# Decoder output product in two column pairs: one between the fourth and fifth projection of a turn, one behind the sixth

## The reference, cut to what matters

```python
x = x + _L0_xattn_ref(_layernorm(x, axis=-1), ctx_4096)          # x: (8, 64, 2048)
x = x + _L0_attn_ref(_layernorm(x, axis=-1), w_q, w_k, w_v, w_o)
x = x + _L0_ffn_ref(_layernorm(x, axis=-1), A_w, B_w, Wq_w, keys)

def _L0_attn_ref(hidden_states, w_q, w_k, w_v, w_o):              # 32 heads, 8 key groups of 4, 128 wide
    q = (hidden_states @ w_q).reshape(B, S, Hkv, g, D)
    k = (hidden_states @ w_k).reshape(B, S, Hkv, D)
    v = (hidden_states @ w_v).reshape(B, S, Hkv, D)
    scores = jnp.einsum('bqhgd,bkhd->bhgqk', q, k) * scale        # causal mask, softmax
    attn = jnp.einsum('bhgqk,bkhd->bqhgd', probs, v)
    return attn.reshape(B, S, Hq * D) @ w_o                       # (512, 4096) @ (4096, 2048)
```

## Time and profile before

| | us |
|---|---|
| median of 3 runs | 1690.09 |
| lowest, highest | 1689.28, 1690.12 |
| profiled execution, its own time | 1688.0 |
| its span, first to last instruction | 1686.1 |

### The profile page before, as it was taken

The page is one execution under the profiler, slowest core; times in us unless marked ns, Lnnn a source line. Parts: engine busy times, 40 slices in busy tenths (PEclk is TensorE's granted clock), DMA queues, the critical chain, the costliest instruction groups (busy, mean ns, idle before and its releaser), DMA issues.

```text
span 1686.1 us, 22552 instructions
## 1 busy us (share of the span) xinstructions
PE 1629.8 (97%) x8893; PEld 1196.6 (71%) x8893; DVE 765.7 (45%) x1331; ACT 554.5 (33%) x784; POOL 490.6 (29%) x155
## 2 busy tenths in 40 slices
PE   6999999999999979999999999999999999999999
PEld 5565565655556558887887878878878878887877
DVE  3464645556464360137156256263371561248433
ACT  2433433443444332233233233332332332322221
POOL 0000000000011004348458366474484583350010
PEclk9999999999999989999999999999999999999999
DMA  9556576675776514322314323224223143220023
GB/s 329 156 202 216 189 240 191 212 227 179 244 232 203 182 53 158 92 76 92 107 51 127 87 85 100 75 75 124 75 91 107 51 148 118 84 100 26 26 75 125
DMA packets 178888, 224.58 MB, mean 133 GB/s; under 512 B 4240, under 2 KB 102544, under 8 KB 176048
## 3 DMA queue, kind: packets, MB, share of 16 engines
q1 hardware_dynamic: 178816, 223.56, 41.4%
HBM read 212.54 MB, written 11.01 MB: 133 GB/s over the span
## 4 chain that ended last, share of the span: by engine, by line
PE 54%; issue 23%; POOL 18%; DVE 2%; ACT 1%; DMA 1%; POOLq 0%; SPq 0%; DVEq 0%
PE ps L623 12%; PE ps L690 11%; POOL w_lo L1149 10%; PE ps L664 10%; POOL w_lo L1156 8%; PE ps L742 5%; PE ps L744 5%; PE ps L743 5%; PE ps L1812 1%; PE ps L635 1%; DMA xa_raw_a<-in_ctx 0%; PE ps L1633 0%; PE ps L1667 0%; PE ps L668 0%; DMA raw<-in_L_attn_w_o 0%
## 5 line engine op out<-in xcount | busy, mean ns | idle before, releaser
L1149 POOL TENSOR_TENSOR w_lo<-raw,w_hi 128x2048 fp32r<-128x2048 f32 x46 | 212.2, 4612 | 421.0 <-ACT w_hi L1203 399.1
L742 PE MATMUL ps<-h_hi,w_hi 128*128 128x512 f32 x800 | 316.5, 396 | 0.0
L744 PE MATMUL ps<-h_hi,w_lo 128*128 128x512 f32 x800 | 311.8, 390 | 0.0
L743 PE MATMUL ps<-h_lo,w_hi 128*128 128x512 f32 x800 | 311.5, 389 | 0.0
L442 ACT ACTIVATE xa_ct<-ps 128x512 f32<-128x512 f32 x256 | 152.8, 598 | 186.6 <-PE ps L623 115.6
L577 DVE COPY xa_ct<-ps 128x321 f32<-128x321 f32 (+1 forms) x256 | 117.5, 459 | 210.8 <-PE ps L623 136.0
L664 PE MATMUL ps<-xa_ct,xa_q_t 128*64 128x384 f32 x1024 | 184.5, 490 | 0.0
L742 PEld LDWEIGHTS ps<-h_hi,w_hi 128*128 128x128 f32 x800 | 150.3, 188 | 35.2 <-ACT sa_q_t L1268 2.0
L744 PEld LDWEIGHTS ps<-h_hi,w_lo 128*128 128x128 f32 x800 | 150.1, 188 | 32.1
L743 PEld LDWEIGHTS ps<-h_lo,w_hi 128*128 128x128 f32 x800 | 150.4, 188 | 29.6
L1143 POOL TENSOR_TENSOR w_lo<-raw,w_hi 128x2048 fp32r<-128x2048 f32 x2 | 9.1, 4542 | 506.9 <-ACT w_hi L1043 506.9
(11 more groups left out here) (236 smaller groups left out, 2312.6 us busy)
## 6 DMA issues: line engine op xcount, KB each, us to landing
xa_raw_a<-in_ctx SPq DMA_DIRECT2D x32, 1536.0 KB
xa_raw_b<-in_ctx SPq DMA_DIRECT2D x32, 1536.0 KB, 6.7
raw<-in_L_attn_w_q SPq DMA_DIRECT2D x32, 1024.0 KB, 5.9
raw<-in_L_attn_w_o SPq DMA_DIRECT2D x30, 1024.0 KB, 5.1
raw<-in_L_attn_w_k SPq DMA_DIRECT2D x8, 1024.0 KB, 5.8
raw<-in_L_attn_w_v SPq DMA_DIRECT2D x8, 1024.0 KB, 5.8
xa_xq<-in_x SPq DMA_DIRECT2D x8, 512.0 KB, 5.1
xa_raw_a<-in_ctx SPq DMA_DIRECT2D x32, 128.0 KB
```

The costliest lines, as they stand in the source:

```text
L742: pe.matmul(out, hi, mov_hi, start=first, stop=False)
L743: pe.matmul(out, hi, mov_lo, start=False, stop=False)
L744: return pe.matmul(out, lo, mov_hi, start=False, stop=last)
L1149: pool.tensor_tensor(w_lo[:, n % 2, :], raw[:, n % 2, :], w_hi[:, n % 2, :].bitcast(F32), ALU.subtract).then_inc(w_lo_done, 1)
```

## The change

The first column pair (j = 0) is multiplied between the fourth projection (q1) and the fifth (q2), the second behind the sixth as before. Everything that feeds it is renumbered for that:

- PE: `output_parts(g, 0)` stands behind `values_transpose(g)`. The fifth and sixth projection now wait also until part 6's results are out of banks 0 and 1.
- SP: the loads come in the order k, q0, v, q1, two chunks of `w_o`, q2, q3, two chunks of `w_o`. q2's load waits for the first pair's four weight sums, q3's for part 6's low copy, and the second pair's chunks for the low copies of q2 and q3.
- ACT: parts 0 and 1 of the first pair are split behind the third projection's result, the other five behind the fourth's, then q2 in two halves and q3 (`split_between`). Parts 0, 1, 2, 6 of the second pair are split behind the fifth's and sixth's result.
- POOL: the low copies follow that order; q2's comes in two halves.
- DVE: all four weight sums of a pair stand ahead of all its additions. The fourth (p = 5) waits for part 1's low copy in place of part 6's.

`heads_high` and `head_lows` stay where they were in their engines' orders.

The diff, without the parts that only renumber:

```diff
...
@@ -981,7 +982,21 @@
-        return done0(g) + NP + PARTS * j + SPLIT_ORDER.index(p) + 1
+        return done0(g) + EARLY_P + (PARTS + 3) * j + SPLIT_ORDER.index(p) + 1
+    def item_no(g, n):
+        if isinstance(g, int) or n < EARLY_P:
+            return done0(g) + n + 1
+        return done0(g) + PARTS + n + 2
+    def load_no(g, n):
+        return n if isinstance(g, int) or n < EARLY_P else n + 2
+    def wo_load(j):
+        return EARLY_P + 4 * j
@@ -1058,9 +1073,10 @@
                     srcs.append(w_q_v[:, :, bass.ds((g * HG + int(what[1])) * HD, HD)])
-            last = isinstance(g, int) and g == LAST
-            for c in (range(n_wo) if last else (0, 2, 1, 3)[:n_wo]):
-                srcs.append(w_o_v[g - 1, :, :, c * 512:(c + 1) * 512])
+            by_parts = not isinstance(g, int)
+            last = n_wo and not by_parts
+            wo = [w_o_v[g - 1, :, :, c * 512:(c + 1) * 512] for c in ((0, 2, 1, 3) if by_parts else range(n_wo))]
+            srcs = srcs[:EARLY_P] + wo[0:2] + srcs[EARLY_P:] + wo[2:4] if by_parts else srcs + wo
             for n, src in enumerate(srcs):
@@ -1068,9 +1084,13 @@
                     sp.wait_ge(w_lo_done, done0(g))
-                elif n == NP + 2 and not last:
+                elif by_parts and n == load_no(g, EARLY_P):
                     sp.wait_ge(t_sums, 1 + TURN_SUMS * (g - 1) + 4)
-                elif n < NP + 2 or last:
+                elif by_parts and n == load_no(g, EARLY_P + 1):
+                    sp.wait_ge(w_lo_done, split_no(g, 0, PARTS - 1))
+                elif by_parts and n >= wo_load(1):
+                    sp.wait_ge(w_lo_done, item_no(g, n - wo_load(1) + EARLY_P))
+                else:
                     sp.wait_ge(w_lo_done, done0(g) + n - 1)
@@ -1144,17 +1164,28 @@
         def turn(g):
-            for n in range(2 if isinstance(g, int) and g == 0 else 0, NP):
-                pool.wait_ge(w_hi_done, done0(g) + n + 1)
-                pool.tensor_tensor(w_lo[:, n % 2, :], raw[:, n % 2, :], w_hi[:, n % 2, :].bitcast(F32),
+            def item(n, part=slice(0, D), more=0):
+                pool.wait_ge(w_hi_done, item_no(g, n) - more)
+                pool.tensor_tensor(w_lo[:, n % 2, part], raw[:, n % 2, part], w_hi[:, n % 2, part].bitcast(F32),
                                    ALU.subtract).then_inc(w_lo_done, 1)
-            if isinstance(g, int):
-                return
-            for j in range(2):
+            def blocks(j):
                 for p in SPLIT_ORDER:
...
                                        ALU.subtract).then_inc(w_lo_done, 1)
+            if isinstance(g, int):
+                for n in range(0 if g else 2, NP):
+                    item(n)
+                return
+            for n in range(EARLY_P):
+                item(n)
+            blocks(0)
+            item(EARLY_P, slice(0, HALF_D), 1)
+            item(EARLY_P, slice(HALF_D, D))
+            item(EARLY_P + 1)
+            blocks(1)
@@ -1208,16 +1239,27 @@
+        def split_between(g):
+            act.wait_ge(w_in[0], 8 * (item0(g) + load_no(g, EARLY_P)) + 16)
+            for k, p in enumerate((3, 4)):
+                act.wait_ge(wo_bank, banks0(g) + 2 * p + 2)
+                part = slice(k * HALF_D, (k + 1) * HALF_D)
+                act.activation(w_hi[:, 0, part], raw[:, 0, part], ACT.Copy).then_inc(w_hi_done, 1)
+            act.wait_ge(w_in[1], 8 * (item0(g) + load_no(g, EARLY_P)) + 16)
+            act.wait_ge(wo_bank, banks0(g) + 2 * PARTS)
+            act.activation(w_hi[:, 1, :], raw[:, 1, :], ACT.Copy).then_inc(w_hi_done, 1)
         def split_half(g, j, p):
             if p in FROM_RAW:
-                act.wait_ge(w_in[FROM_RAW[p][0]], 8 * (item0(g) + NP + 2 * j) + 16)
+                act.wait_ge(w_in[FROM_RAW[p][0]], 8 * (item0(g) + wo_load(j)) + 16)
             else:
...
             same, q = HELD_BY[p]
-            if same or j:
-                act.wait_ge(wo_bank, banks0(g) + 2 * (PARTS * (j - 1 + same) + q) + 2)
+            if same:
+                act.wait_ge(wo_bank, banks0(g) + 2 * (PARTS * j + q) + 2)
             else:
-                act.wait_ge(proj_done, NP * g + NP - 1 + PLACE_OF[p] // 2)
+                act.wait_ge(proj_done, NP * g + EARLY_P - 1 + 2 * j + PLACE_OF[p] // 2)
             act.activation(half_slot(w_hi, p), half_source(p), ACT.Copy).then_inc(w_hi_done, 1)
@@ -1283,9 +1325,13 @@
                     act.activation(keys_t[:], ps_wq[0:RD, DC * RD:DC * RD + EXPERTS], ACT.Copy).then_inc(wq_hi, 1)
-                if by_parts and n + 2 >= NP:
-                    for p in SPLIT_ORDER[2 * (n + 2 - NP):][:2]:
-                        split_half(g, 0, p)
+                if by_parts and n + 2 >= EARLY_P:
+                    for p in SPLIT_ORDER[n % 2 * 2:][:2]:
+                        split_half(g, (n + 2 - EARLY_P) // 2, p)
+                    if n == EARLY_P - 1:
+                        for p in SPLIT_ORDER[4:]:
+                            split_half(g, 0, p)
+                        split_between(g)
                 else:
@@ -1293,8 +1339,6 @@
                 for p in SPLIT_ORDER[4:]:
-                    split_half(g, 0, p)
-                for p in SPLIT_ORDER:
                     split_half(g, 1, p)
@@ -1451,7 +1495,7 @@
                 for n in range(2):
-                    dve.wait_ge(w_in[n], 8 * (item0(g) + NP + 2 * j) + 16)
+                    dve.wait_ge(w_in[n], 8 * (item0(g) + wo_load(j)) + 16)
             dve.wait_ge(w_lo_done, split_no(g, 0, p) if j else done0(g))
@@ -1463,7 +1507,7 @@
-                dve.wait_ge(w_lo_done, split_no(g, j, PARTS - 1))
+                dve.wait_ge(w_lo_done, split_no(g, j, 1))
                 dve.tensor_tensor(t1, b12, b11, ALU.subtract).then_inc(t_sums, 1)
@@ -1492,15 +1536,12 @@
             head_lows(g)
-            for p in (2, 3, 4):
-                weight_sum(g, 0, p)
-            for i in range(WO_HALVES):
-                for r2 in range(2):
-                    add_part(g, i, r2)
-                if i == 1:
-                    weight_sum(g, 0, 5)
-                if PARTS - 3 <= i <= PARTS:
-                    weight_sum(g, 1, i - PARTS + 5)
+            for j in range(2):
+                for p in (2, 3, 4, 5):
+                    weight_sum(g, j, p)
+                for i in range(PARTS * j, PARTS * (j + 1)):
+                    for r2 in range(2):
+                        add_part(g, i, r2)
@@ -1637,9 +1678,10 @@
         def project(g, n):
-            n0 = done0(g)
             slot = n % 2
-            pe.wait_ge(w_lo_done, n0 + n + 1)
+            pe.wait_ge(w_lo_done, item_no(g, n))
+            if not isinstance(g, int) and n >= EARLY_P:
+                pe.wait_ge(wo_added, evac_no(g, PARTS - 1, n - EARLY_P))
@@ -1709,9 +1751,11 @@
             if i == 0:
-                pe.wait_ge(proj_out, NP * (g + 1) - 1 + r2)
+                pe.wait_ge(proj_out, NP * g + EARLY_P - 1 + r2)
                 if r2 == 0:
                     pe.wait_ge(a_lo_done, 3 * g)
+            if i == PARTS + 1:
+                pe.wait_ge(proj_out, NP * (g + 1) - 1 + r2)
             if r2 == 0:
@@ -1745,6 +1789,11 @@
             i.then_inc(wo_bank, 1)
+        def output_parts(g, j):
+            for i in range(PARTS * j, PARTS * (j + 1)):
+                for r2 in range(2):
+                    times_w_o_part(g, i, r2)
@@ -1767,6 +1816,8 @@
             values_transpose(g)
+            if not isinstance(g, int):
+                output_parts(g, 0)
             project(g, 4)
@@ -1775,9 +1826,7 @@
             if kind(g)[1]:
-                for i in range(WO_HALVES):
-                    for r2 in range(2):
-                        times_w_o_part(g, i, r2)
+                output_parts(g, 1)
```

More of the change, by code:

```diff
@@ L758 @@
 WO_HALVES = 2 * PARTS
-TURN_W = NP + WO_HALVES
+EARLY_P = 4
+TURN_W = NP + 1 + WO_HALVES
 TURN_BANKS = 2 * WO_HALVES
```

## The result

| | before | after |
|---|---|---|
| median of 4 runs, us | 1690.11 | 1722.88 |
| lowest, highest | 1689.28, 1690.37 | 1721.76, 1724.65 |
| span of the profiled execution | 1686.1 | 1720.4 |
| mean granted clock of PE | 0.996 | 0.984 |

The changed kernel takes 1.0196 times as long (95% interval 1.0178 to 1.0213): 32.8 us slower. The forecast was 1725, with 1712 to 1739 as the range.

A forecast was written before the change was run, and what follows sets the result against it. TensorE, busy 97%, was taken as the bound, with 4.95 us a turn to win. A 6.35 + B 3.3 + C 0.9 + restarts = 10.85, less 4.95: +5.9 a turn, +35.4 us, 1725 us (range 1712 to 1739).

The forecast's parts named there:

- What bounds the kernel: TensorE is busy 97% of the span; the output product loses 4.95 us a turn, all that can be won.
- it gets faster: Rival: heads' low copies ready by 853.8 and sums made before; -3.95 us a turn, 1666 us; chance 4%.
- Term A: First pair's start: PE waits after the fourth projection for DVE's low copies of the heads, 6.35 us a turn.
- Term B: Parts 0 to 3 of the first pair: part 3 waits for POOL's low copy, two DVE collisions included, 3.3 us.
- rival with a small B: POOL and DVE don't meet, part 3's delay is 1.2 us; +3.8 to +4.7 a turn, 1713 to 1718; 17%.
- The projections behind: Fifth and sixth projections after the first pair: q2's low copies are ready 1.5 us ahead, so no cost.
- Term C: Second pair: part 3 starts 9.06 us after part 0 in place of 8.16, costing 0.9 us a turn.
- The sum: 10.85 us a turn added, 4.95 removed: net +5.9 a turn, +35.4 us over six turns.
- three restarts at 0.1: PE's restarts after waits, three a turn at 0.1 us each, added to the turn's cost.
- The clock: PE's clock falls at the first pair's stop each turn; the 2.1 us lost is hidden by part 3's wait.
- The sign I gave: PE should wait 3 us a turn for POOL's low copies at part 3 of the first pair.
- the rival that I built on it: Low clock not hidden: +2.1 us a turn, +12.4 us, 1738; 15% together with a late q2 low copy.

The follow-up runs named there:

- The version with the heads early: Changed kernel with the heads' whole path moved up (values' products into and behind the second projection, high copies before the third's copy-out): 1668.04 us, ratio 0.987.
- the first run above: Changed kernel with ACT making the heads' three high copies ahead of its copy-out of the fourth projection: 1704.61 us, ratio 1.0091.
- The filled stop: Changed kernel with 25 extra matmuls a turn between the transposes of v and the first part: 1733.94 us, ratio 1.0264.
- the two edits together: Changed kernel with the 25 extra matmuls and the first pair's third and fourth weight sums cut to 8 columns: 1712.53 us, ratio 1.0133.

## Why the prediction was right

*What bounds the kernel*: the loss of 4.95 us a turn as the most that can be won was the right frame. The version with the heads early, at a turn of 112.57, took 3.4 of it. That is also the case that the prediction gave as "it gets faster" (1666) and tied to the heads' copies being ready: with them ready it came, at 1668.

*Term A*, 6.35 us: 6.43 measured. The whole path was in the rows of before, since the change moves none of it; the first run above moved one step of the path by 3.4 us and the first pair moved by as much. The sum of heads ended at 977.9, ahead of the copy-out at 980.84, so it cost nothing, as I had it.

*Term B*, 3.3: 3.2 measured. Two collisions at 1.0 each, as taken; POOL's first low copy starts 2.2 us behind the pair's first matmul where I had 2.4. With the collisions taken away and the clock kept up, part 3 came 9.43 us after part 0, which is a B of 1.26 where the prediction had 1.2 for this case, and the turn was 3.8 us longer than before, as it had for its rival with a small B.

*The projections behind*: the fifth starts at 1009.82, straight behind part 6's last matmul (1009.59), without a wait; q2's second low copy ends at 1008.68, 1.1 us ahead where I had 1.5. *Term C*, 0.9: 0.91.

*The sum*: +5.9 a turn, measured +5.73; 35.4 against 34.3 in the span. The median moved by 32.8. One of the three restarts at 0.1 was counted twice: the one behind the first stop lies inside B, which is measured up to part 3's start. The measured loss of 10.68 less A, B and C leaves 0.15 for restarts, not 0.3.

*The clock* was the weakest step. That it falls in each turn and that this costs nothing came out: low for 3.0 to 5.4 us behind the restart where I took 4.4, and 1.4 to 2.5 us taken out of a wait of 2.9, where I had 2.1 out of 3.3. The sign I gave, a wait of 3 us at part 3, did not fit my own sum, which left 1.2 of it beside a low clock; 0.37 to 1.53 were measured. The Trainium skill ("TensorE: Matmul & The Clock Gate", section "HAM oscillation — how this bites in real kernels") has a wait inside a loop drop the clock anew each time, and the trace agrees, six times in six. But the rival that I built on it, +12.4 us if it isn't hidden, supposed that it could only become worse by lasting longer. The filled stop shows what I did not have: at the wait that hides the low clock, the clock falls itself when there is nothing to hide. That the changed kernel's time was not touched by it is in part luck.

## What to carry to other kernels

Before a block of work is moved up on the engine that bounds a kernel, list what it waits for and which of these waits the moved-over work covered; here two projections of 21.9 us had hidden a path that ends 6.3 us behind the fourth one, and the move was worth having only with that path moved too. A wait taken off one engine's queue is no gain until the next queue behind it has been looked at. And where PE stands for some microseconds anyway, filling the stop with idle work can cost time, as it did here by 11 us, because the clock then fell at the next stop.

## What was not expected of the hardware

The clock's fall isn't decided by the length of the stop alone. Waits of 2.4 to 2.5 us never dropped it in the kernel before (1.00 over the output product in all six turns), nor did waits of 2.4 to 2.65 us in the kernel before with early heads; waits of 2.4 to 2.6 us dropped it in five turns of six with the sums one place later, 2.8 us dropped it in five of six turns with the heads' high copies early, and 2.9 us in all six with the stop filled. So the "stop of some 3 us or more" in my expectation for the two edits together doesn't hold as a rule. What else decides it isn't settled by these runs. Low stretches behind a restart took 1.4 to 2.5 us from PE.
